# Deformable-conv layer, offsets stage: where the turns of the pixel-major copy stand in the order

## What is computed

```python
def deform_conv(x, offset, w, b):
    ...
    py = base_y.astype(x.dtype) + dy
    px = base_x.astype(x.dtype) + dx
    sampled = bilinear_gather(x, py, px)
    return jnp.einsum('bckhw,ock->bohw', sampled, w.reshape(O, C, K2)) + b[None, :, None, None]
s0 = deform_conv(x, conv3x3(x, off_w0, off_b0), dw0, db0)
s1 = deform_conv(x, conv3x3(x, off_w1, off_b1), dw1, db1)
```

## Time and profile before

| | |
|---|---|
| Time, median of 3 runs | 1556.57 us (1553.92 to 1556.88) |
| Profiled execution | 1555.91 us, its span 1554.1 us |
| Mean granted clock of TensorE | 0.906 of 2.4 GHz |
| Busy, share of the span | TensorE 79%, VectorE 68%, ScalarE 41%, GpSimd 27% |
| `offsets1` in the span | from about 329 to 434 us |
| `windows1` in the span | from about 437 us |

### The profile page before, as it was taken

One profiled execution on the slowest core, in us unless ns is written; L12 is line 12 of the kernel. 1 busy time (PEld: TensorE's weight loads), 2 busy tenths in 40 slices (PEclk: granted clock), 3 DMA queues, 4 the chain that ended last, 5 costly groups with the idle time before them and its releaser, 6 DMA issues. The chain is left out here.

```text
span 1554.1 us, 32058 instructions
## 1 busy us (share of the span) xinstructions
PE 1233.8 (79%) x13604; PEld 609.2 (39%) x13604; DVE 1058.1 (68%) x1310; ACT 638.8 (41%) x1003; POOL 418.1 (27%) x272
## 2 busy tenths in 40 slices
PE   3850099947559999999999977659999999999558
PEld 1430077723214444444444444413333333334323
DVE  2769945645568888888888866684666667677723
ACT  1434035423335555555555533704444444445410
POOL 2001021121200000000000000307888888888500
PEclk9985599968759999999999997788999999999879
DMA  4000000011100000000000000310000000000032
GB/s 80 15 1 0 1 2 4 2 45 27 23 26 27 27 27 27 26 27 27 27 24 25 24 10 0 78 45 1 1 1 2 1 2 1 2 2 2 31 53 63
DMA packets 29071, 31.50 MB, mean 20 GB/s; under 512 B 19340, under 2 KB 21837, under 8 KB 28157
## 3 DMA queue, kind: packets, MB, share of 16 engines
q1 hardware_dynamic: 28925, 29.41, 7.8%
HBM read 21.07 MB, written 5.35 MB: 17 GB/s over the span
## 5 line engine op out<-in xcount | busy, mean ns | idle before, releaser
L2069 POOL TENSOR_TENSOR arena_sb<-arena_sb 128x768 f32<-128x768 f32 x168 | 323.0, 1922 | 121.2 <-ACT arena_sb L2030 100.6
L2084 DVE TENSOR_REDUCE arena_sb<-ps 128x4 f32<-128x1536 f32 x108 | 188.2, 1756 | 129.4 <-PE ps L1926 128.6
L2030 ACT ACTIVATE arena_sb<-ps 128x768 f32<-128x768 f32 x216 | 174.9, 811 | 242.6 <-PE ps L1959 240.5
L1473 PE MATMUL ps<-xp_sb,arena_sb 32*120 32x384 f32 x1728 | 206.5, 548 | 25.1 <-DVE arena_sb L1580 22.0
L1585 DVE TENSOR_TENSOR arena_sb<-ps,arena_sb 120x768 f32<-120x768 f32 x216 | 206.8, 957 | 8.3 <-DVE arena_sb L1580 0.8
L1959 PE MATMUL ps<-arena_sb 33*64 33x384 f32 x1728 | 187.6, 502 | 11.4 <-ACT arena_sb L2030 5.5
L1491 PE MATMUL ps<-arena_sb 120*64 120x216 f32 x1536 | 182.1, 359 | 0.0
L1971 PE MATMUL ps<-arena_sb 64*64 64x384 f32 x1728 | 168.1, 488 | 3.4 <-ACT arena_sb L2037 3.4
L1543 ACT ACTIVATE arena_sb<-ps 120x384 f32<-120x384 f32 x216 | 106.2, 492 | 148.1 <-PE ps L1473 148.1
L1580 DVE COPY arena_sb<-ps 120x384 f32<-120x384 f32 x216 | 120.5, 558 | 42.9 <-PE ps L1473 40.1
L1762 POOL MEMSET arena_sb<- 128x64 f32 x1 | 0.2, 152 | 543.9 <-POOLq L210 543.9
(11 more groups left out here) (228 smaller groups left out, 1497.3 us busy)
## 6 DMA issues: line engine op xcount, KB each, us to landing
arena_sb<-pixel_major SPq DMA_DIRECT2D x96, 120.0 KB, 2.3
pixel_major<-arena_sb SPq DMA_DIRECT2D x24, 108.0 KB
x_sb<-in_x SPq DMA_DIRECT2D x4, 576.0 KB, 8.5
arena_sb<-arena_sb SPq DMA_DIRECT2D x8, 288.0 KB, 6.0
xn_sb<-in_W SPq DMA_DIRECT2D x1, 2304.0 KB, 8.3
arena_sb<-in_W SPq DMA_DIRECT2D x1, 2304.0 KB, 8.1
out_x<-x_sb SPq DMA_DIRECT2D x24, 96.0 KB, 2.2
arena_sb<-arena_sb SPq DMA_DIRECT2D x16, 36.0 KB, 3.7
```

The costliest lines, as they stand in the source:

```text
L1473: mm = pe.matmul(out, k["spr"][32 * row:32 * row + 32, q, :], hat[32 * row:32 * row + 32, slot, :], start=True, stop=True)
L2030: act.activation(pt[g % SLOTS].rearrange("p (h n) -> p h n", h=2), p_scores(g), ACT.Exp)\
L2069: pool.tensor_tensor(acc, first, pt[g % SLOTS], ALU.add).then_inc(S["pool_added"], 1)
L2084: v.tensor_reduce(part.rearrange("p (a u j) -> p a u j", a=3, u=NB)[:, a, :, jc], p_m(m), AX.X, ALU.max)\
```

## The change

The turns of a pair move one iteration on. In iteration n TensorE does five taps of conv n (instead of four), the turns of pair n-1, the other four taps and the spread of n-1. The turns and the spread of the last pair follow behind the loop. `turn` now waits for the additions of all pairs ahead of its own (`y >= 4 n`), and `spread` for the copies of its own pair (`pp >= 2 n + 2`). On ScalarE the copies of pair n+1 move from the head of iteration n to its end, behind the second four casts; in the first iteration `keep` stands ahead of the copies. The lists of VectorE, GpSimd and SP stay as they are.

```diff
--- before.py
+++ after.py
@@ -1193,8 +1193,8 @@
                 pe.wait_ge(S["xs"], m + 1)
                 if m >= 2:
                     pe.wait_ge(S["pp"], m - 1)
-                if n >= 2:
-                    pe.wait_ge(S["y"], 4 * (n - 1))
+                if n:
+                    pe.wait_ge(S["y"], 4 * n)
                 for t in range(NTP):
                     mm = pe.transpose(p_x[m % 2][:, 128 * t:128 * t + 128], xs[m % 2][:, TP * t:TP * t + TP],
                                       k["ident"][:, :])
@@ -1202,7 +1202,7 @@
 
             def spread(b2, i, n):
                 pe.wait_ge(S["raw"], 2 * (n + 1))
-                pe.wait_ge(S["pp"], min(2 * n + 4, 2 * CPI))
+                pe.wait_ge(S["pp"], 2 * n + 2)
                 if n:
                     pe.wait_ge(S["y"], 4 * n)
                 for h, c in four:
@@ -1211,12 +1211,15 @@
                 mm.then_inc(S["rep_ps"], 1)
 
             for b2, i, n in pairs:
-                conv(b2, i, n, range(0, 4))
-                turn(n, 2 * n)
-                turn(n, 2 * n + 1)
-                conv(b2, i, n, range(4, TAPS))
+                conv(b2, i, n, range(0, 5))
+                if n:
+                    turn(n - 1, 2 * n - 2)
+                    turn(n - 1, 2 * n - 1)
+                conv(b2, i, n, range(5, TAPS))
                 if n:
                     spread(*pairs[n - 1])
+            turn(len(pairs) - 1, 2 * CPI - 2)
+            turn(len(pairs) - 1, 2 * CPI - 1)
             spread(*pairs[-1])
 
         @block.scalar
@@ -1235,12 +1238,9 @@
 
             for b2, i, n in pairs:
                 if n == 0:
+                    keep(b2, i, n)
                     copied(0)
                     copied(1)
-                    keep(b2, i, n)
-                if n + 1 < len(pairs):
-                    copied(2 * n + 2)
-                    copied(2 * n + 3)
                 for q in range(2):
                     for e, (h, c) in enumerate(four):
                         if q == 0:
@@ -1250,6 +1250,9 @@
                         act.activation(hi[h][c], y[h][c], ACT.Copy).then_inc(S["hi"], 1)
                     if q == 0 and n + 1 < len(pairs):
                         keep(*pairs[n + 1])
+                if n + 1 < len(pairs):
+                    copied(2 * n + 2)
+                    copied(2 * n + 3)
 
         @block.vector
         def _(v):
```

## The result

| | before | changed |
|---|---|---|
| Time, median | 1556.27 us (1553.92 to 1556.88, 4 runs) | 1518.80 us (1518.78 to 1519.66, 4 runs) |
| Profiled execution, span | 1555.91, 1554.1 us | 1518.79, 1517.0 us |
| Ratio to before | | 0.9763, 95% interval 0.9746 to 0.9780 |
| Additions of a pair to the next (starts on VectorE) | 16.75, 16.91, 16.99, 17.02, 7.46 us | 8.61, 8.62, 8.61, 8.62, 9.10 us |
| First additions, last additions | 351.76, 426.89 us | 344.96, 388.52 us |

These are the stretches of the changed kernel that answer to the earlier trace rows, cut at the first addition of each pair. The columns are the length; the busy time of PE, PEld, DVE, ACT and POOL with the number of records; the clock; the DMA share; and GB/s.

A forecast was written before the change was run, and what follows sets the result against it. In the offsets stage VectorE and TensorE took turns, 8.5 + 8.5 = 17.0 us a pair. Gains of 5.3 (opening) and 33.2 (four long periods) less 0.4 (last pair) made 38.1 us, so 1518 us, range 1511 to 1530.

The forecast's parts named there:

- The ring: Offsets stage, middle pairs: TensorE's spread, five taps, turns and four taps sum to 8.61 us a period, over VectorE's 8.51.
- The clock term: TensorE in the four middle periods: 8.6 us if all at clock 1.00, 11.6 with today's low stretches; 8.61 taken.
- The wait for the additions: TensorE before the turns: additions end at 3.54 us, TensorE arrives at 4.86, so no cost, 1.3 us to spare.
- The copies: ScalarE behind the second casts: done at 7.9 us, TensorE reaches the spread at 8.61, so covered by 0.7 us.
- The opening: Start of the offsets stage: first additions at 346.44 instead of 351.76, a gain of 5.3 us.
- The last pair: End of the offsets stage: 7.9 us instead of 7.46, as turns and copies now precede its spread; loss 0.4 us.
- first rival: Offsets stage: TensorE's clock keeps dropping, 11.6 us of work a period, about 1530 us; chance 0.12.
- The sum: Whole kernel: 5.3 + 33.2 - 0.4 = 38.1 us gained, profiled execution 1517.8, median forecast 1518 us.
- The rivals: Whole kernel, four other outcomes: clock keeps dropping 0.12, next stage wakes earlier 0.07, nothing gained 0.02, slower 0.02.
- wake earlier: Stage after the offsets: clock rises at once, up to 5.8 us more gained over about nine slow passes, 1512; chance 0.07.
- the signs named: Profile checks: additions 8.5 to 8.7 us apart, clock 1.00, VectorE's spread wait some 4 us, next stage near 399.
- The rule against it: TensorE's clock: frequent tiny pauses between matmul groups make it swing, so each period keeps its low stretch; 1530 us.

## Why the prediction was right

- **The ring.** "TensorE's ring is 1.48 + 3.38 + 1.02 + 2.73 = 8.61 us" and "I take 8.61": measured 8.61 to 8.62 four times. From the first additions to the fifth it took 34.46 us instead of the 67.67 before; forecast 34.44. That TensorE's ring decides, and not VectorE's 8.51, was shown by leaving out GpSimd's casts. The clock term held too: 1.00 in all four stretches, and filling the idle time of the kernel before showed its price, 2.8 us a pair.
- **The wait for the additions** "costs nothing, with 1.3 us to spare". TensorE did not idle before the turns in the four pairs, and with one tap less ahead of them nothing changed.
- **The copies** were "covered by 0.7 us". They end 0.96 us ahead of the spread, and the tripled copies showed 0.86 us of cover. The term was mis-sized at "some 6.3 us after the additions start": its own rows add up to 5.09 + 1.09 = 6.18, and the copies ended 6.06 us after them.
- **The opening.** "Gain 5.3 us" was 6.8 in the profiled execution, since the clock rose earlier than in the trace before. From the stage's first matmul to the first additions the kernel before took 22.82 us, and the forecast amounts to 17.50. The changed kernel took 15.85, and eight other profiles of kernels with this opening (one with a tap less ahead of the turns) 15.92 to 17.62. So the gain is 5.2 to 7.0 us by execution. I had taken one execution's clock there for a constant.
- **The last pair.** "Loss 0.4" was 1.64. The step that failed is "6.3 + 1.59 = 7.9 us": 6.06 until the copies are done was near enough, but TensorE had idled 2.14 and 3.01 us by then, the clock fell, and from the last spread's start to the additions it took 2.94 us instead of 1.59. The trace before had shown this. Its last spread stood behind a pause too, and took 2.42 us instead of 1.54:

```profile
422.94 2.42 PE L1209 MATMUL ps<-arena_sb 64*108 64x384 f32 x8 [3.55 <-ACT arena_sb L1227]
```

It also contradicts the prediction's argument against its first rival, that each fall of the clock came "behind an idle stretch of over 5 us": this pause was 3.55 us long.

- **Behind the stage** nothing was to change, and 1.2 us were lost in this execution, mostly where the clock rose later.
- **The sum.** 5.3 + 33.2 - 0.4 = 38.1 us against 6.8 + 33.2 - 1.6 = 38.4 at the last additions, and 37.1 in the execution. The opening was 1.5 us better than forecast, the last pair and what follows the stage 1.2 us worse each. That 1518 came out within a microsecond is in part luck: these errors happened to cancel. That the time fell by some 38 us is not, since 33.2 of them are the four long periods, forecast to 0.02 us.
- **The rivals.** The clock kept its full level in all four long periods. The next stage did not wake earlier: its first nine passes are slow in both kernels, and in the changed one the clock's later rise cost 0.6 us. Of the signs named, VectorE's wait for the spread (some 4 us) was 5.1, and the next stage's start (near 399) 398.9. ScalarE's copies waited for nobody but once, 2.7 us in the opening.
- **The rule against it**, from the page "TensorE: Matmul & The Clock Gate" of the Trainium skill, would have given 1530 and wasn't borne out in this kernel, nor with one short pause in each period: 0.36 to 1.02 us (two taps less) and 1.01 us (copies tripled) left the granted clock at 1.00. With copies ahead of the casts one period of 11.3 us had 0.85. TensorE had paused once in it, for 2.01 us ahead of the turns, while the next period, with two pauses of 1.01 and 0.59 us, had 1.00. So in these runs the low stretches came behind single pauses of 2 us and more, and not behind many small ones; not each pause of that length had one.

## What to carry to other kernels

When two engines each work for half of a period, look for the step that ties this period's work on one to this period's work on the other, and run it one iteration later; then write the ring of every engine from durations taken at full clock, since the low clock in the rows may itself be a product of the wait. The waits that this adds have to be checked on all the engines: the same turns with copies ahead of the casts gave only 21 of 38 us. The ends of such a pipeline, where the overlap is missing, are worth a look of their own once its middle is full.

## What was not expected of the hardware

VectorE's subtractions slow down beside GpSimd's casts. In the changed kernel eight take 4.81 us and the four casts 2.83; without the casts eight take 4.31. With two taps left out it was the other way round in the four middle pairs: 4.30 us for the subtractions and, in the pair shown above, 4.19 for the casts. The page "GPSIMD Engine Reference" of the Trainium skill (Specifications) says that GpSimd's way to SBUF is shared with VectorE and contended where VectorE has two inputs there, as these subtractions have. The trace agrees that the two collide; which of them pays, and why it changed with TensorE's work, no run here settles.

The clock's rises and falls come at other moments in each execution. The same opening took 15.85 to 17.62 us from its first matmul to the first additions, and repeated runs of the changed kernel lay between 1516.48 and 1523.84 us. In the filled kernel one of four equal periods got a low stretch (0.89 over the period), though TensorE's pause ahead of the turns was 2.15 us in each of them.
